# An attention and mixture-of-experts layer on one core: load order, w1 in eight pieces, the last two tiles together, the last expert by 128 tokens

## The reference, cut to what matters

```python
mod = (silu(c) @ wmod).reshape(4, 6, 1, 128)         # sa, ca, ga, sb, cb, gb
ga = sign(ga) * maximum(abs(ga), 0.25)               # gb the same
h = layernorm(x) * (1 + ca) + sa
x = x + ga * attention(h)                            # 16 heads, 4 kv heads, D 64
h = layernorm(x) * (1 + cb) + sb
x = x + gb * moe(h)
# attention: scores = 30 * tanh(q k / (8 * 30)), key j seen by query i if i-128 < j <= i
# moe: 8 experts, each token to its best expert, at most 512 tokens an expert,
#      out = gate * (relu(t @ W1[e] + b1[e]) @ W2[e] + b2[e]); tokens beyond 512 get 0
```

## Time and profile before

| | us |
|---|---|
| median of 3 runs | 476.98 (475.44 to 479.21) |
| the profiled execution, its own time | 476.81 |
| its span | 475.1 |
| PE busy | 417.4 (88%) |
| POOL busy | 310.8 (65%) |
| ACT busy | 298.0 (63%) |
| DVE busy | 286.9 (60%) |

### The profile page before, as it was taken

How to read it: one execution, slowest core, us unless ns; L and a number is a source line. 1 busy time by engine, 2 the same in 40 slices (tenths; PEclk the granted TensorE clock), 3 DMA queues, 4 the chain that set the end, 5 groups by cost and what they waited for, 6 DMA issues and landing times. The chain is left out here.

```text
span 475.1 us, 14910 instructions
## 1 busy us (share of the span) xinstructions
PE 417.4 (88%) x5608; PEld 294.0 (62%) x5608; DVE 286.9 (60%) x846; ACT 298.0 (63%) x537; POOL 310.8 (65%) x494
## 2 busy tenths in 40 slices
PE   2894999999999999999999999999999742899970
PEld 1652566766767676666677666767565531799960
DVE  6263557775676868576777756675777541245631
ACT  4785457777776868777777778676756221564420
POOL 6136248587786969687867878676769851055572
PEclk9998899999999999999999999999999765999995
DMA  8987000101101010102011110101020125971110
GB/s 261 369 294 231 3 23 3 41 25 37 52 20 54 20 52 20 43 19 70 20 52 38 35 41 21 52 20 52 21 86 24 42 96 188 364 248 39 33 50 16
DMA packets 32078, 37.73 MB, mean 79 GB/s; under 512 B 3474, under 2 KB 28311, under 8 KB 32008
## 3 DMA queue, kind: packets, MB, share of 16 engines
q1 hardware_dynamic: 28936, 28.22, 19.1%
q0 software_dynamic: 3072, 8.56, 5.0%
HBM read 15.88 MB, written 17.31 MB: 70 GB/s over the span
## 5 line engine op out<-in xcount | busy, mean ns | idle before, releaser
L1185 POOL TENSOR_TENSOR OL<-O,OH 128x512 fp32r<-128x512 f32 x64 | 81.3, 1285 | 22.3 <-ACT OH L701 21.8
L865 DVE COPY_PREDICATED own<-before,turns 128x1024 f32<-128x1024 uint32 x56 | 68.8, 1229 | 40.3 <-PE turns L424 40.3
L689 ACT ACTIVATE PR<-own 128x1024 f32<-128x1024 f32 x64 | 65.5, 1024 | 42.4 <-DVE own L865 42.0
L1177 POOL TENSOR_SCALAR_AFFINE_SELECT PM<-PR 128x1024 f32<-128x1024 f32 x64 | 69.5, 1096 | 22.4 <-ACT PR L695 22.0
L695 ACT ACTIVATE PR<-PR 128x1024 f32<-128x1024 f32 x64 | 65.8, 1054 | 0.0
L420 PE MATMUL own<-Q,K 64*32 64x256 f32 (+3 forms) x896 | 58.8, 441 | 1.9 <-ACT PR L689 1.7
L896 DVE TENSOR_TENSOR O<-turns,R 128x512 f32<-128x512 f32 x64 | 41.2, 685 | 29.2 <-PE turns L463 28.9
L424 PE MATMUL turns<-Q,K 64*32 64x128 f32 (+3 forms) x896 | 57.4, 429 | 0.0
L701 ACT ACTIVATE OH<-O 128x512 fp32r<-128x512 f32 x64 | 40.0, 628 | 11.0 <-DVE O L896 10.9
L1221 POOL DMA_INDIRECT sorted_rows<-PAY,slot_i x32 | 35.1, 1096 | 14.0 <-issue 10.9
L424 PEld LDWEIGHTS turns<-Q,K 64*32 64x32 f32 x896 | 36.5, 107 | 9.4
(11 more groups left out here) (189 smaller groups left out, 1010.8 us busy)
## 6 DMA issues: line engine op xcount, KB each, us to landing
sorted_rows<-PAY SPq DMA_DIRECT2D x8, 800.0 KB, 12.1
VM<-V SPq DMA_DIRECT2D x56, 64.0 KB, 2.1
x_sb<-x_dram SPq DMA_DIRECT2D x4, 512.0 KB, 6.7
w_stage<-w_dram SPq DMA_DIRECT2D x1, 2048.0 KB, 10.9
out_dram<-PAY SPq DMA_DIRECT2D x32, 64.0 KB, 1.7
x_sb<-sorted_rows SPq DMA_DIRECT2D x2, 800.0 KB, 9.6
Q<-sorted_rows SPq DMA_DIRECT2D x2, 800.0 KB, 9.1
PR<-sorted_rows SPq DMA_DIRECT2D x2, 800.0 KB
```

What stands on the lines that cost most here:

```text
L689: act.activation(pr, own[:, :, :].rearrange("p a n -> p (a n)"), ACT.Tanh, scale=SCORE_SCALE).then_inc(tanhed, 1)
L865: dve.copy_predicated(own[:, :, :].rearrange("p a (r n) -> p (a r) n", n=P), before[:, :].bitcast(U32).unsqueeze(1).to_broadcast([P, 2 * R ...
L1177: pool.affine_select(out=PM[:, u % P_RING, :].rearrange("p (r n) -> p r n", n=P), in_=PR[:, u % P_RING, :].rearrange("p (r n) -> p r n", n ...
L1185: pool.tensor_tensor(OL[:, t % 2, c, :], O[:, t % 2, c, :], OH[:, t % 2, c, :].bitcast(F32), ALU.subtract).then_inc(ol_done, 1)
```

## The change

It does these things.

- **Load order.** SP loads x of the first two tiles, wk, the second half of wq, the first half of wq, wv, the rest of batch 0; then waits for POOL's constants and issues the eight transfers of empty rows; then wo, x of batches 1 to 3, Wg, b1. ACT issues c and wmod (in two halves) itself. ACT and DVE split in the order K, Q1, Q0, V, and `normalise1(0)`, `normalise1(1)` and `high_x(0)` stand between the splits.
- **Empty row.** It is a tile of its own, and the waits for `empty_in` go from ACT, DVE and `name_row` to the first `scatter`. A row is 388 numbers in place of 400, in the order H, ID, G, X.
- **w1.** Eight transfers of 256 KB, one in every second tile from tile 8 on, in place of one of 2 MB ahead of the first `mix_v`.
- **High parts first.** `out_project` runs the 16 matmuls with OH after a wait for OH, then the 8 with OL after the wait for OL.
- **Last two tiles.** Tiles 30 and 31 leave the loops at `turn_y`; behind the loops each step is done for both, one step after the other, and `rstd2` for both in one instruction. They get PSUM banks of their own.
- **Warm.** Behind `count(31)` PE runs five matmuls of 512 columns in fp32 whose result is not used.
- **Last expert.** x + gate * b2 is made ahead (`prepare_last`), and down, gate, add and scatter go by 128 tokens, with two DVE instructions of 128x128 each.

```diff
-ROW_H, ROW_G, ROW_X, ROW_ID, ROW = 0, P, 2 * P, 3 * P, 400
+ROW_H, ROW_ID, ROW_G, ROW_X, ROW = 0, P, P + 4, 2 * P + 4, 3 * P + 4
+def in_turn(t):
+    return 0 <= t < TILES - 2
...
         def program_sp(sp):
-            sp.dma_start(x_sb[:, 0:BATCH_TILES, :], x_v[0]).then_inc(x_in[0], 16)
-            sp.dma_start(cT[:, :], c).then_inc(c_in, 16)
-            sp.dma_start(stage_m, wmod).then_inc(wmod_in, 16)
+            sp.dma_start(x_sb[:, 0:2, :], x_v[0][:, 0:2, :]).then_inc(x_first, 16)
             sp.dma_start(stage_k, wk).then_inc(wk_in, 16)
+            sp.dma_start(stage_q[:, QH:], wq[:, QH:]).then_inc(wq1_in, 16)
+            sp.dma_start(stage_q[:, :QH], wq[:, :QH]).then_inc(wq0_in, 16)
             sp.dma_start(stage_v, wv).then_inc(wv_in, 16)
-            sp.dma_start(stage_q, wq).then_inc(wq_in, 16)
+            sp.dma_start(x_sb[:, 2:BATCH_TILES, :], x_v[0][:, 2:BATCH_TILES, :]).then_inc(x_in[0], 16)
+            sp.wait_ge(consts, CONSTS)
+            for e in range(EXPERTS):
+                sp.dma_start(sorted_v[e], empty_row[:, :].unsqueeze(1).to_broadcast([P, ST, ROW])).then_inc(empty_in, 16)
+            sp.dma_start(stage_o, wo.rearrange("p (i n) -> p i n", n=P)).then_inc(wo_in, 16)
             for b in range(1, BATCHES):
                 sp.dma_start(x_sb[:, b * BATCH_TILES:(b + 1) * BATCH_TILES, :], x_v[b]).then_inc(x_in[b], 16)
-            sp.dma_start(stage_o, wo.rearrange("p (i n) -> p i n", n=P)).then_inc(wo_in, 16)
             sp.dma_start(Wg[:, :], wg).then_inc(rest_in, 16)
             sp.dma_start(b1_col[:, :, :], b1).then_inc(rest_in, 16)
-            sp.wait_ge(consts, CONSTS)
-            for e in range(EXPERTS):
-                sp.dma_start(sorted_v[e], empty_row.unsqueeze(1).to_broadcast([P, ST, ROW])).then_inc(empty_in, 16)
...
-            sp.dma_start(w1_sb, w1.rearrange("e h f -> h e f")).then_inc(w1_in, 16)
+            def load_w1(e):
+                if e == 0:
+                    sp.wait_ge(weights_l, len(split))
+                    sp.wait_ge(columns_done, 1)
+                    sp.wait_ge(rows_done, 1)
+                sp.dma_start(w1_sb[:, e, :], w1[e]).then_inc(w1_in, 16)
...
                 if is_tile(e + 24):
                     mix_v(e + 24)
+                if W1_TILE <= e + 14 < W1_TILE + 2 * EXPERTS:
+                    load_w1((e + 14 - W1_TILE) // 2)
...
         def program_pe(pe):
...
-                pe.wait_ge(ol_done, 4 * k + 4)
-                y = ps[:, 0:BT]
+                y = ps[:, 0:BT]
+                pe.wait_ge(oh_done, 4 * k + 4)
                 for i in range(2 * REP):
-                    oh, ol = (o[:, :, :, i * HALF:(i + 1) * HALF] for o in (OH, OL))
+                    oh = OH[:, :, :, i * HALF:(i + 1) * HALF]
                     pe.matmul(y, WoH[:, i, :], oh, start=(i == 0), stop=False)
-                    pe.matmul(y, WoH[:, i, :], ol, start=False, stop=False)
-                    last = pe.matmul(y, WoL[:, i, :], oh, start=False, stop=(i == 2 * REP - 1))
+                    pe.matmul(y, WoL[:, i, :], oh, start=False, stop=False)
+                pe.wait_ge(ol_done, 4 * k + 4)
+                for i in range(2 * REP):
+                    last = pe.matmul(y, WoH[:, i, :], OL[:, :, :, i * HALF:(i + 1) * HALF], start=False, stop=(i == 2 * REP - 1))
...
+            for t in LAST_TWO:
+                turn_y(t)
+            for t in LAST_TWO:
+                turn_h2(t)
+            for t in LAST_TWO:
+                score_experts(t)
+            for t in LAST_TWO:
+                count(t)
+            n, ps = take("warm")
+            for i in range(5):
+                pe.matmul(ps[:, :], ident[:, :], mod[:, :, :, :].rearrange("p b j n -> p (b j n)")[:, 0:512], start=True, stop=True)
...
+            def down_last():
+                e = EXPERTS - 1
+                pe.wait_ge(w2_in[e], 16)
+                pe.wait_ge(relu_done, FC * (e + 1))
+                for s in range(ST):
+                    if s < 2:
+                        pe.wait_ge(b2_added, 2 * (e - 1) + s + 1)
+                    for f in range(FC):
+                        last = pe.matmul(last_banks[s][:, 0:P], hidden[e % 2][:, f, s * P:(s + 1) * P], w2_sb[e][:, f, :],
+                                         start=(f == 0), stop=(f == FC - 1))
+                    last.then_inc(down_done, 1)
...
         def program_act(act):
...
+            act.dma_start(cT[:, :], c).then_inc(c_in, 16)
+            act.dma_start(stage_m[:, 0:3 * P], wmod[:, 0:3 * P]).then_inc(wmod_in, 16)
+            act.dma_start(stage_m[:, 3 * P:6 * P], wmod[:, 3 * P:6 * P]).then_inc(wmod2_in, 16)
...
             split_high(SPLIT_K)
+            normalise1(0)
+            normalise1(1)
+            split_high(SPLIT_Q1)
+            high_x(0)
             split_high(SPLIT_Q0)
             split_high(SPLIT_V)
-            split_high(SPLIT_Q1)
...
                 if e == -12:
                     split_high(SPLIT_O1)
                     split_high(SPLIT_O0)
                 if is_tile(e + 12):
                     keep_v(e // 2 + 6)
...
         def program_dve(dve):
...
+            def finish_last():
...
+                for s in range(ST):
+                    dst = done_rows[e % 2][:, s, :]
+                    dve.wait_ge(down_done, 2 * e + s + 1)
+                    dve.tensor_tensor(dst, last_banks[s][:, 0:P], rows[e][:, s, ROW_G:ROW_G + P],
+                                      ALU.mult).then_inc(g_scaled, 1)
+                    dve.wait_ge(g_scaled, 2 * e + s + 1)
+                    dve.tensor_tensor(dst, dst, more[:, s, :], ALU.add).then_inc(x_added, 1)
...
         def program_pool(pool):
...
+            pool.wait_ge(mv2_done, TILES)
+            pool.tensor_scalar(var2[:, s], mv2[:, s, 1], EPS, 1.0, ALU.add, ALU.mult).then_inc(var2_done, 2)
+            pool.wait_ge(var2_done, TILES)
+            pool.tensor_tensor(rstd2[:, s], var2[:, s], neg_half[:, :], ALU.pow).then_inc(rstd2_done, 2)
+            for t in LAST_TWO:
+                mark(t)
+                add_seen(t)
+            for t in LAST_TWO:
+                number_slot(t)
+                scatter(t)
```

More of the change, by code:

```diff
@@ L60 @@
 }
+LAST_HOME = {("y", 0): 0, ("y", 1): 2, ("h2", 0): 3, ("h2", 1): 4, ("logits", 0): 5, ("logits", 1): 0, ("count", 0): 3, ("count", 1): 4}
 def is_tile(t):
     return 0 <= t < TILES
+def in_turn(t):
+    return 0 <= t < TILES - 2
 def first(t):
@@ L244, in build @@
         down_banks = [turns[:, n, :] for n in (4, 5)]
+        last_banks = [turns[:, n, :] for n in (4, 5, 0, 1)]
         bank = {}
@@ L629, in program_pe @@
             up(EXPERTS - 1)
-            down(EXPERTS - 1)
+            down_last()
         def program_act(act):
@@ L802, in program_act @@
                     expose(e + 12, 0)
+            for t in LAST_TWO:
+                keep_h2(t)
+            for t in LAST_TWO:
+                exp_gate(t)
+            for t in LAST_TWO:
+                gate_row(t)
             def split_w1(e):
@@ L1089, in program_dve @@
                     spread(e + 12)
+            for t in LAST_TWO:
+                add_x(t)
+                measure2(t)
+                gather2(t)
+            for t in LAST_TWO:
+                normalise2(t)
+                modulate2(t)
+                shift2(t)
+            for t in LAST_TWO:
+                keep_logits(t)
+                top8(t)
+                which(t)
+                negate(t)
+            for t in LAST_TWO:
+                locate(t)
+                invert_gate(t)
             def low_w1(e):
@@ L1124, in program_dve @@
                 finish(e - 1)
+            prepare_last()
             finish(EXPERTS - 2)
-            finish(EXPERTS - 1)
+            finish_last()
         def program_pool(pool):
@@ L1211, in name_row @@
                     pool.wait_ge(pay_out[r], 16 * (t // PAY_RING))
-                else:
-                    pool.wait_ge(empty_in, 16 * EXPERTS)
                 pool.tensor_copy(PAY[:, r, ROW_ID:ROW_ID + 1].bitcast(I32), tok_id[:, t:t + 1]).then_inc(id_done, 1)
@@ L1217, in scatter @@
                 r = t % PAY_RING
+                if t == 0:
+                    pool.wait_ge(empty_in, 16 * EXPERTS)
                 pool.wait_ge(id_done, t + 1)
```

163 lines of the change are left out of this document (94 added, 69 removed).

## The result

The changed kernel takes 484.0 us (median of 4, 482.9 to 486.6) where the kernel before takes 476.2: the ratio is 1.0171, 95% interval 1.0135 to 1.0206. It is slower by 1.7%; the forecast was 473.8, and 484.0 lies above the range.

A forecast was written before the change was run, and what follows sets the result against it. PE's work bounds the long middle, so only the two ends can change. Start +1.5, tail edits -1.5, warm -1.2 and last expert -2.0 sum to -3.2: 473.8 us median, range 461 to 479 including rival A.

The forecast's parts named there:

- Cost 0; without that cover 1.4 us a piece: Middle: 256 KB pieces of w1 delay only VM copies, asked for three tiles ahead, so they cost nothing.
- Start: Start of kernel: hole removed -8.85, ACT's stall for wo +7.0, half clock +3.3; together +1.5, from -2.5 to +5.5.
- That stall covers all: Start: ACT's wait for wo hides the front's gain of perhaps 2 us, so that gain counts 0.
- 7.25 + 17.0 + 1.4 + 0.7 = 26.4 us: Start: landing of wo, from loads ahead, empty rows at 373 GB/s, wo itself and reporting; bounds 25.5 to 28.
- C: Rival, first two tiles: clock stays at half until attend(1), start +12.1, whole kernel 485.9 us; chance 0.06.
- A: Rival, start: empty rows don't hold wo back, ACT never stalls, start -10.9, whole kernel 461.2 us; chance 0.13.
- B: Rival, kernel's end: DVE's late last release goes, another -3.9, whole kernel 469.9 us; chance 0.10.
- High parts first and the last two tiles: Last out_project to last scatter into sorted rows: both edits together -1.5 us, from -4.0 to +1.5.
- I count 11.3: Last two tiles: turn_y(30) to the last scatter takes 11.3 us side by side, against 12.1 half overlapped.
- Warm: Between last count and first expert: unused matmuls bring the clock to full, -1.2 us, from -2.3 to +0.5.
- Last expert: Kernel's end: fewer DVE instructions and one scatter after the last release, -2.0 us, from -1.2 to -2.5.
- so I keep that delay: Kernel's end: DVE's last release, 4 us late for an unnamed reason, stays as late.

The follow-up runs named there:

- e4: Kernel before with w1 as eight transfers, one to an expert, in place of one; 465.93 us, 0.990 of before.
- e2: Changed kernel with only wo moved ahead of the eight empty rows; 479.84 us, 1.020 of before.
- e3: Changed kernel with only x of batch 1 moved ahead of the eight empty rows; 479.36 us, 1.019 of before.
- e1: Changed kernel with x of batches 1 to 3, wo, Wg and b1 ahead of the empty rows; 466.81 us, 0.992 of before.
- e5: e1 with the last two tiles in turn, as in the kernel before; 466.27 us, 0.978 of before.
- e6: e1 with the last two tiles side by side, but tile 29's count, locate, number_slot and scatter behind turn_y; 466.86 us, 0.979 of before.
- e8: The kernel of e1 run again, unchanged, as base for e5 to e7; 469.12 us, 0.986 of before.
- e7: e1 without the five 512-column matmuls of warm; 470.76 us, 0.985 of before.
- e9: e5 with the last expert as in the kernel before; 461.42 us, 0.982 of before.
- e10: e5 with PE waiting for DVE's last x_added at the end of its program; 462.26 us, 0.982 of before.
- e14: The kernel of e10 run again, unchanged; 462.95 us, 0.984 of before.
- e16: Kernel before with PE waiting for DVE's last x_added at the end of its program; 476.13 us, 1.001 of before.

## Why the prediction was wrong, point by point

**What bounds the kernel.** Right: the middle is PE's, the ends decide. The conclusion drawn from it, that nothing moved into the middle can be seen unless it changes PE's work, was a failure of its own. The sentence "Cost 0; without that cover 1.4 us a piece" named VM as the only one who shares the queue with w1. The stores of PAY share it too, and their ring had no time left: DVE already waited for it four times before. The stretch grew by 1.7 us in the changed kernel, and by 2 to 3 in e4.

**Start.** Two steps failed. One is the order "x of batches 1 to 3", not looked at where the text says "That stall covers all". The prediction followed one transfer, wo, past the empty rows. x of batch 1 was moved past them too, and was needed at about 16 us by DVE, in order, ahead of a low part that PE waits for. e2 and e3 show that it is a gate of its own and as late as wo. The other is a term that was mis-sized, "7.25 + 17.0 + 1.4 + 0.7 = 26.4 us" for the landing of wo: it was 29.19. The sum took 373 GB/s throughout; from 24 to 30 us, with reads behind the writes, the rate was 300. The 0.7 us to report have no row. The Trainium skill (DMA: Bandwidth & Descriptors, "Anatomy of one DMA") fits 2.0 us and the bytes over 436 GB/s to transfers that GpSimd issues; these are issued by SP. With its 436 GB/s wo would have been there 2.4 us before the 26.4; the trace doesn't agree, with 29.19. The first scores came at 34.04 and not at 29.8. In e3, which takes the gate of x away, they start 3.45 us behind the split of wo (33.83 and 30.38). By that distance, as an estimate, wo alone would have brought them to 32.6 in the changed kernel: 2.8 of the 4.2 us are wo's landing, and 1.4 the gate of x. From there to `attend(1)` it was 1.2 us more than the prediction had: 55.27 instead of 49.8. The start was +7.1 at tile 2, not +1.5. Its bounds, -2.5 and +5.5, don't quite follow from their parts, which give -1.8 and +5.2.

**The sum of the misses.** From the predicted 473.6 to the 486.55 of the profiled execution it is 12.9 us: start 5.6, middle 1.7, last tiles 1.8, warm 1.8, last expert 1.7, together 12.6; 0.3 more is the time outside the span. All five terms missed in the same direction.

**The rivals.** C gave 485.9 and the time came near it, but what it told did not happen: the clock was back by 38.6 us, before its mark of 42: that its number lies near is luck. A, wo not late, is what e1 makes true. It gave 461.2; e1 has 0.986 to 0.992 of before, 469.5 to 472.4 by that measure, since neither w1's cost nor the missing gains of the tail were in it. B, the late release goes, did not happen on the chip of the first runs.

**High parts first and the last two tiles.** The projection's gain was right: in the changed kernel it starts 0.98 us behind the last OH instead of 3.03, and runs at a clock of 0.68 (0.51 before). The sum's sign for the rest was not. `turn_y` came at 391.10, 9.07 us after the last OH, where the prediction had 8.5; the chain behind it took 12.44 instead of the 11.3 that was estimated without a row, against 12.08 in turn before. -1.5 became +0.28. The steps that failed are "I count 11.3" (1.1 us) and "I get about 3.7 us of them" (0.6 us). e5 and e6 show that the part gains nothing behind `turn_y`, and e5 and the other runs in turn that it costs 3.2 to 3.7 us, as much as the projection had won.

**Warm.** -1.2 was near the right size where the clock holds (-1.4 in the profile of e8 against that of e7). The changed kernel's profile has +0.64, where it fell again: the possibility that the term's upper bound, +0.5, stood for. That the clock would stay up was the step that failed.

**Last expert.** -2.0 became -0.33 in the changed kernel. What it was made of came out: from DVE's last release to the last scatter it was 3.42 us before and is 1.42 now. The step that failed is "so I keep that delay": the release stayed late, as forecast, but came 9.58 us behind the start of the last down and not 7.91. Where there is no late release, on the other chips, the part gains nothing, for another reason: POOL's scatters follow each other without a gap, and one that is taken off DVE's path is not off POOL's.

**The front.** First projection at 13.39 against 13.30: counted 0, and 0.

All versions of the changed kernel with the loads in the old order beat both kernels. The fastest against before have the tiles in turn too: e5 (0.978), e9 (0.982), e10 and e14 (0.982 and 0.984), with w1 in pieces, high parts first and warm.

## What to carry to other kernels

When a transfer is put ahead of others, list every transfer that it passes and, for each, the first instruction that wants it and all that stands behind that instruction on its engine; two loads that are late side by side hide each other, and moving one alone is worth next to nothing. When a transfer's landing is summed up from a rate, the sum is only as good as the rate that was measured for that mix of transfers. Small transfers slipped into a steady loop are not free because one consumer has slack: look for the ring with the shortest slack, which shows as short waits already. Before a last result is brought forward, see whether the engine that takes it is idle then.

## What the runs showed of the hardware

Chips differ in more than a constant. Before takes 476 to 477 us on the chip of e5 to e8 and e16 and in the first runs, and 470 to 471 on four others; by pieces, the 6 us are 2.2 to 4 between tile 2 and tile 30 (302.4 and 302.9 against 298.9 to 300.2) and 3.2 at the very end, where matmuls whose starts the profile puts 0.11 us apart are released by groups, in `down_last` at intervals of 2.9 us and more for eight instead of 0.9. The profile's modelled ends don't show it; only DVE's waits do. Its cause is open, and it isn't the DRAIN at the end of PE's program.
